# Conv stage: q product in the image's natural order, bias data on ScalarE's queue, bias and value products among the energies

## The chip, the core and the metric

One core of a Trainium2 chip runs the whole program. The metric is the device time of one execution, in microseconds, as the median of several runs. TensorE (PE in the rows) multiplies; its weight loads are the rows PEld. VectorE is DVE, ScalarE is ACT, GpSimd is POOL, and SyncE (SP) only issues DMAs here. ScalarE issues a few DMAs too.

## What is computed

The input is `x`, 4 images of 128 channels and 16 x 16 pixels. A convolutional attention comes first, then an attention over tokens with 8 heads, then a dense mixture of 8 experts. Only the first stage is touched:

```
q = einsum('bchw,oc->bohw', x, wq) + bq          # 16 channels
k = einsum('bchw,oc->bohw', x, wk) + bk          # 16 channels
v = einsum('bchw,oc->bohw', x, wv) + bv          # 128 channels
qf, kf = q.reshape(b, 16, h*w), k.reshape(b, 16, h*w)
energy = einsum('bci,bcj->bij', qf, kf).reshape(b, h, w, h, w)
attn = softmax(energy, axis=-1)
out  = einsum('bchk,bhwkv->bcwv', v, attn)
x    = gamma * out + x
```

(The literal reshape of the reference is `(b, c // 8, h * w)`, with c // 8 = 16.) All later stages need the result of this one.

## The kernel before

The program is written out by hand, one instruction stream for each engine, with semaphores between them. What stands in a stream in a row runs in that order; there is no scheduler. So the order on an engine is the order of the code in that engine's block.

The tokens of all images lie side by side, 1024 columns; a half `p` (512 columns) is two images. `x_sb` is the input with the channels on the partitions, in natural order, row `h` outside and column `w` inside. `dev` holds at first a second copy of the input in another order, for the values.

The stage goes like this:

- SyncE issues the loads: the two halves of `x_sb` (L282), the value bias `bv_sb` (L283, one row of 128 numbers sent to all 128 partitions), `dev`, the constants, the attention weights, then the experts' weights. ScalarE issues `convw_sb`, the weights of the three products (L414), `convb_sb`, the biases of q and k (L415), and `gamma_sb` (L416, one number sent to 128 partitions).
- TensorE first runs `turn`, matmuls on zeros whose result nobody reads (L855, 128x512, type f32r). Then, for each half, it makes the q product (L863, 16 output channels on PSUM partitions 64 to 79) and two k products (L867, PSUM partitions 0 to 15 and 32 to 47). L863 reads `x_sb` with `w` outside and `h` inside, so neighbouring columns of the product are 16 numbers (64 bytes) apart in `x_sb`. The last L867 of a half signals `proj_done`.
- ScalarE and VectorE copy the products out of PSUM and add the bias. Both wait for `convb_in` once and for `proj_done` of the half. ScalarE writes q for the first row group (L425), then k (L427). VectorE writes k (L585), waits for ScalarE's q copy of the half (`act_cq_ready`), and writes q for the second row group (L588).
- `conv_bias(i)` (L898) is the product that puts the value bias into PSUM bank 4 + i, `energy(q)` (L878) makes 16 products of one quarter of the energies, and `conv_values(i)` (L887) adds four value products to bank 4 + i. `energy(0)` waits for all copies of q and k; `conv_bias(0)` waits for `bv_in`; `conv_values(0)` waits for `xk_in`, the data in `dev`.
- The softmax of a quarter q: VectorE takes the maximum (L595) and subtracts it (L597), ScalarE takes the exponential (L431), VectorE sums (L603) and inverts (L606); GpSimd scales quarters 0 to 2 (L333), VectorE scales quarter 3 (L611). ScalarE copies the values out of PSUM (L522) between its exponentials.
- `conv_apply(0)` and `conv_apply(1)` (L910) multiply values and attention. The first needs the copied values and GpSimd's quarter 1, the second needs `last_A_ready`, VectorE's L611. L632 then makes the stage's output.

Most matmuls here are fp32, and the profile has two records for each fp32 matmul.

Of the kernel before, what the change touches and what calls it, by code (L numbers as in the profile page):

```python
# [19 lines left out]
B, C, H, W = 4, 128, 16, 16  # L20
# [4 lines left out]
C8 = C // 8  # L25
# [6 lines left out]
WQ, W4 = 4, 4  # L32
# [10 lines left out]
def hybrid_program(nc, x_in, xk_in, convw, convb, bv, gamma, attw, gate, w1, w2, b1, b2, consts, out):  # L43
# [5 lines left out]
    with ExitStack() as ctx:  # L49
        def sb(name, shape, dt=f32):  # L50
            return ctx.enter_context(nc.sbuf_tensor(name, shape, dt))

        def sem(name):
            return ctx.enter_context(nc.semaphore(name))
# [7 lines left out]
        convw_sb = sb("convw_sb", [128, QK + C])  # L62
        convb_sb = sb("convb_sb", [96 + C8, 1])
        bv_sb = sb("bv_sb", [128, C])
# [16 lines left out]
        x_sb = sb("x_sb", [128, T])  # L81
# [16 lines left out]
        cq = room[0:32 + C8, 5120:7168].rearrange("p (b w h k) -> p b w h k", b=B, w=W, h=H)  # L98
# [45 lines left out]
        PS = ctx.enter_context(nc.psum_tensor("PS", [128, 8, 512], f32))  # L144
# [5 lines left out]
        convb_in, bv_in, czero, tzero = sem("convb_in"), sem("bv_in"), sem("czero"), sem("tzero")  # L150
# [40 lines left out]
        def cols(p):  # L191
            return slice(p * HALF, (p + 1) * HALF)

# [75 lines left out]
        def weigh_visit(n):  # L272

            for k in range(VISITS):
                if n == MT * k + WEIGH_LAG - 2 * (k > E):
                    return k
            return None

        @block.sync
        def _(sp):  # L280
            for p in range(NHALF):
                sp.dma_start(x_sb[:, cols(p)], x_in[:, cols(p)]).then_inc(x_in_s[p], 16)  # L282
            sp.dma_start(bv_sb[:, :], bv.partition_broadcast(128)).then_inc(bv_in, 16)  # L283
            sp.dma_start(dev[:, :], xk_in).then_inc(xk_in_s, 16)
            sp.dma_start(cst[:, :], consts).then_inc(cst_in, 16)
            sp.dma_start(attw_sb[:, :], attw).then_inc(attw_in, 16)

            for e in range(2):
                sp.dma_start(w1raw[e][:, :], w1[:, e * HID:(e + 1) * HID]).then_inc(w1_in[e], 16)

            sp.dma_start(gate_sb[:, :], gate).then_inc(cst_in, 16)
            sp.dma_start(b2_sb[:, :], b2).then_inc(cst_in, 16)
            sp.dma_start(b1_sb[:, :], b1).then_inc(cst_in, 16)

            def comb_everywhere(p, part):

                if part == 0:
                    sp.wait_ge(combT_ready, p + 1)
                    sp.dma_start(comb_rows_dram[p], combT[:, cols(p)]).then_inc(comb_out, 16)
                    sp.wait_ge(comb_out, 16 * (p + 1))  # L300
                for e in range(E)[part * E // 2:(part + 1) * E // 2]:
                    if p:
                        sp.wait_ge(part_ready, e + 1)
                    sp.dma_start(combB[:, e, :], comb_rows_dram[p, e, :].partition_broadcast(128))\
                        .then_inc(combB_in[e], 16)

            for e in range(2, E):
                sp.dma_start(w1raw[e][:, :], w1[:, e * HID:(e + 1) * HID]).then_inc(w1_in[e], 16)
            for n in range(2):
                half = slice(n * E // 2, (n + 1) * E // 2)  # L310
                sp.dma_start(w2_sb[:, half, :], w2[:, half, :]).then_inc(w2_in[n], 16)
            for p in range(NHALF):
                comb_everywhere(p, 0)
                comb_everywhere(p, 1)

            for p in range(NHALF):
                sp.wait_ge(acc_done, E * (p + 1))
                sp.dma_start(out[:, cols(p)], t2[:, cols(p)]).then_inc(out_sent, 16)
            sp.wait_ge(out_sent, 16 * NHALF)
# [92 lines left out]
        @block.scalar  # L412
        def _(act):
            act.dma_start(convw_sb[:, :], convw).then_inc(convw_in, 16)  # L414
            act.dma_start(convb_sb[:, :], convb).then_inc(convb_in, 16)  # L415
            act.dma_start(gamma_sb[:, :], gamma.partition_broadcast(128)).then_inc(gamma_in, 16)  # L416

# [4 lines left out]
            for p in range(NHALF):  # L422
                act.wait_ge(proj_done, p + 1)
                pair = slice(2 * p, 2 * p + 2)
                nc.scalar.activation(cq[0:C8, pair, :, :, 0].rearrange("c b w h -> c (b w h)"), PS[64:64 + C8, p, :],  # L425
                                     ACT.Identity, bias=convb_sb[64:64 + C8, 0:1]).then_inc(act_cq_ready, 1)
                nc.scalar.activation(ck[32:32 + C8, pair, :], PS[32:32 + C8, p, 0:TOK].rearrange("c (b n) -> c b n", b=2),  # L427
                                     ACT.Identity, bias=convb_sb[32:32 + C8, 0:1]).then_inc(ck_ready, 1)
# [146 lines left out]
        def _(dve):  # L575
# [6 lines left out]
            for p in range(NHALF):  # L582
                dve.wait_ge(proj_done, p + 1)
                pair = slice(2 * p, 2 * p + 2)
                nc.vector.tensor_scalar(ck[0:C8, pair, :], PS[0:C8, p, 0:TOK].rearrange("c (b n) -> c b n", b=2),  # L585
                                        convb_sb[0:C8, 0:1], None, ALU.add).then_inc(ck_ready, 1)
                dve.wait_ge(act_cq_ready, p + 1)
                nc.vector.tensor_scalar(cq[32:32 + C8, pair, :, :, 1].rearrange("c b w h -> c (b w h)"),  # L588
                                        PS[64:64 + C8, p, :], convb_sb[64:64 + C8, 0:1], None, ALU.add)\
                    .then_inc(cq_ready, 1)  # L590

            def shift(q):
# [220 lines left out]
            for n in range(STEPS):  # L813
# [12 lines left out]
                k = weigh_visit(n)  # L826
# [22 lines left out]
        def _(pe):  # L849
            mm = nc.tensor.matmul  # L850

            def turn(count, bank=6):

                for _ in range(count):
                    mm(PS[:, bank, :], spin[:, 0:128], spin, start=True, stop=True)  # L855
# [4 lines left out]
            for p in range(NHALF):  # L860
                pe.wait_ge(x_in_s[p], 16)
                x2 = x_sb[:, cols(p)].rearrange("c (b g n) -> c g b n", b=2, g=K2N)
                mm(PS[64:64 + C8, p, :].rearrange("c (b w h) -> c b w h", b=2, w=W),  # L863
                   convw_sb[:, 0:C8], x_sb[:, cols(p)].rearrange("c (b h w) -> c b w h", b=2, h=H),
                   start=True, stop=True)
                for g in range(K2N):
                    last = mm(PS[32 * g:32 * g + C8, p, 0:TOK].rearrange("c (b n) -> c b n", b=2), convw_sb[:, C8:QK],  # L867
                              x2[:, g], start=True, stop=True)
                last.then_inc(proj_done, 1)

            def energy(q):
                if q == 0:
                    pe.wait_ge(act_cq_ready, NHALF)
                    pe.wait_ge(cq_ready, NHALF)
                    pe.wait_ge(ck_ready, 2 * NHALF)
                for w in range(W4):
                    for b in range(B):
                        last = mm(PS[32 * b:32 * (b + 1), q, w * K8 * W:(w + 1) * K8 * W],  # L878
                                  cq[:, b, W4 * q + w, :, :].rearrange("c h k -> c (h k)"), ck[:, b, :],
                                  start=True, stop=True)  # L880
                last.then_inc(energy_done, 1)

            def conv_values(i):
                if i == 0:
                    pe.wait_ge(xk_in_s, 16)
                for k in range(4 * i, 4 * i + 4):
                    last = mm(PS[:, 4 + i, (k % 4) * C:(k % 4 + 1) * C], x_k[:, k, :], convw_sb[:, QK:QK + C],  # L887
                              start=False, stop=True, skip_group_check=True)
                    if k % 4 == 1:
                        turn(1)  # L890
                last.then_inc(vT_done, 1)

            def conv_bias(i):

                if i == 0:
                    pe.wait_ge(share_ready, 1)
                    pe.wait_ge(bv_in, 16)
                mm(PS[:, 4 + i, :].rearrange("p (a c) -> p a c", c=C), share[:, :],  # L898
                   bv_sb[:, :].unsqueeze(1).broadcast_to([128, 4, C]), start=True, stop=False, skip_group_check=True)
# [289 lines left out]
                mm(y, w2h[e][:, ms], Gl[:, n % GR, :], start=False, stop=(m == MT - 1)).then_inc(down_done, 1)  # L1189


            turn(1)
            for i in range(2):
                conv_bias(i)
            for q in range(WQ):
                energy(q)
                turn(1)
            for i in range(2):
                conv_values(i)
            turn(2)  # L1200
            conv_apply(0)
            turn(1, 0)
            conv_apply(1)
# [134 lines left out]
```

## Time and profile before

| | |
|---|---|
| runs | 186.39 us median of 3 (186.04 to 187.66) |
| profiled execution | 186.13 us, of it 184.2 us span |
| TensorE busy | 174.1 us, 95% of the span |
| VectorE, ScalarE, GpSimd busy | 117.1, 123.2, 79.5 us |
| the conv stage | from the start to L632 at 23.29 us |

The span is what the trace covers; 1.93 us lie around it. Times of rows count from the start of the span. A busy share says how often an engine had something to do, not whether the end waited for it: for that there is the chain of work that ended last.

### The profile page before, as it was taken

How to read it: one execution, taken by the hardware profiler on the slowest of the kernel's cores; microseconds unless marked ns; L12 is line 12 of the kernel's file. 1: busy time of each engine (PE TensorE's matmuls, PEld its weight loads, DVE VectorE, ACT ScalarE, POOL GpSimd, SP SyncE). 2: the span in 40 equal slices, each digit the busy share in tenths (PEclk: the TensorE clock that was granted, in tenths of full speed). 3: DMA queues.
4: the chain of work that ended last, by engine and by line, in shares of the span. 5: the costliest groups of instructions: out<-in, count | busy, mean ns of one | idle time of the engine just before them, and what ended most of it. 6: DMA issues, size and time to landing. Idle time of an engine off the chain costs nothing.

```text
span 184.2 us, 3336 instructions
## 1 busy us (share of the span) xinstructions
PE 174.1 (95%) x1277; PEld 118.6 (64%) x1277; DVE 117.1 (64%) x199; ACT 123.2 (67%) x185; POOL 79.5 (43%) x68
## 2 busy tenths in 40 slices
PE   6999999989898998999999999999999999999991
PEld 3267867665466544447466567567887888888880
DVE  1569544985465396456084959397888677676673
ACT  3516953317727743545988598867878999999970
POOL 8404228988703284452536093524151152333312
PEclk9999999999999999999999999999999999999999
DMA  5799200000000000570000000000000880000001
GB/s 141 276 374 419 96 0 0 4 0 4 0 5 0 2 0 4 181 271 7 0 0 5 0 0 0 4 0 0 0 7 4 244 269 0 0 4 0 0 0 57
DMA packets 5791, 10.94 MB, mean 59 GB/s; under 512 B 1280, under 2 KB 1664, under 8 KB 5520
## 3 DMA queue, kind: packets, MB, share of 16 engines
q1 hardware_dynamic: 5360, 10.65, 16.7%
q8 instruction: 10, 0.16, 0.3%
q10 hardware_dynamic: 416, 0.08, 0.3%
q14 instruction: 5, 0.04, 0.1%
HBM read 10.17 MB, written 0.56 MB: 58 GB/s over the span
## 4 chain that ended last, share of the span: by engine, by line
PE 73%; issue 8%; ACT 7%; POOL 4%; DVE 4%; DMA 2%; ACTq 0%; DVEq 0%; POOLq 0%
PE PS L1159 9%; PE PS L1163 7%; PE PS L1160 7%; PE PS L1186 6%; PE PS L1189 6%; PE PS L1187 6%; PE PS L1181 4%; POOL pairs L357 4%; PE PS L1017 3%; PE PS L1031 3%; ACT room L516 2%; PE PS L910 2%; PE PS L878 2%; PE PS L1104 2%; DMA convw_sb<-convw 2%
## 5 line engine op out<-in xcount | busy, mean ns | idle before, releaser
L516 ACT ACTIVATE room<-PS,b_sb 128x512 f32<-128x512 f32 x64 | 43.6, 688 | 22.6 <-PE PS L1163 21.2
L772 DVE TENSOR_TENSOR Gl<-room,Gh 128x512 fp32r<-128x512 f32 x50 | 41.2, 831 | 13.7 <-ACT Gh L461 13.0
L365 POOL TENSOR_TENSOR x_sb<-x_sb,room 128x512 f32<-128x512 f32 x15 | 23.6, 1572 | 56.0 <-DVE room L781 56.0
L1159 PE MATMUL PS<-x2h,w1h 128*128 128x512 f32 x64 | 27.4, 427 | 1.2 <-ACT room L516 0.8
L461 ACT ACTIVATE Gh<-room 128x512 fp32r<-128x512 f32 x40 | 25.3, 633 | 1.3
L1163 PE MATMUL PS<-x2l,w1h 128*128 128x512 f32 x64 | 25.5, 398 | 0.0
L1160 PE MATMUL PS<-x2h,w1l 128*128 128x512 f32 x64 | 25.2, 393 | 0.0
L1186 PE MATMUL PS<-Gh,w2h 128*128 128x512 f32 x50 | 20.8, 416 | 0.0
L1187 PE MATMUL PS<-Gh,w2l 128*128 128x512 f32 x50 | 19.8, 395 | 0.0
L1189 PE MATMUL PS<-Gl,w2h 128*128 128x512 f32 x50 | 19.7, 395 | 0.0
L1159 PEld LDWEIGHTS PS<-x2h,w1h 128*128 128x128 f32 x64 | 12.0, 187 | 10.6 <-issue 4.9
L348 POOL TENSOR_TENSOR w2l<-w_sb,w2h 128x512 fp32r<-128x512 f32 x8 | 10.2, 1279 | 12.6 <-ACT w2h L455 12.6
L357 POOL TENSOR_TENSOR pairs<-shared_probs 128x512 f32<-128x512 f32 x10 | 13.7, 1390 | 4.6 <-ACT shared_probs L503 4.6
L1163 PEld LDWEIGHTS PS<-x2l,w1h 128*128 128x128 f32 x64 | 12.0, 188 | 3.5 <-DVE x2l L718 0.6
L682 DVE TENSOR_REDUCE other_nmx<-PS 128x4 f32<-128x1024 f32 x8 | 9.8, 1224 | 6.7 <-PE PS L1031 6.7
L1181 PE MATMUL PS<-room,w_sb 128*128 128x512 f32 x28 | 14.0, 592 | 0.0
L1160 PEld LDWEIGHTS PS<-x2h,w1l 128*128 128x128 f32 x64 | 12.0, 188 | 2.0
L767 DVE CAST Gh<-room 128x512 fp32r<-128x512 f32 x10 | 4.4, 444 | 13.5 <-ACT room L516 13.5
L503 ACT ACTIVATE shared_probs<-PS 128x1024 f32<-128x1024 f32 x12 | 11.6, 1022 | 1.9 <-PE PS L1074 1.7
L781 DVE SCALAR_TENSOR_TENSOR room<-PS,b_sb,room 128x512 f32<-128x512 f32 x16 | 11.9, 744 | 0.7 <-PE PS L1189 0.7
L373 POOL TENSOR_TENSOR ny<-nv,half_power 128x2 f32<-128x2 f32 (+1 forms) x6 | 4.9, 811 | 15.1 <-DVE nv L651 14.4
L1187 PEld LDWEIGHTS PS<-Gh,w2l 128*128 128x128 f32 x50 | 9.4, 188 | 2.6 <-issue 0.5
(136 smaller groups left out, 294.2 us busy)
## 6 DMA issues: line engine op xcount, KB each, us to landing
room<-comb_rows SPq DMA_DIRECT2D x16, 256.0 KB, 5.2
w1raw<-w SPq DMA_DIRECT2D x8, 256.0 KB, 5.9
w_sb<-w SPq DMA_DIRECT2D x2, 1024.0 KB, 10.6
x_sb<-x SPq DMA_DIRECT2D x2, 256.0 KB, 3.2
dev<-xk SPq DMA_DIRECT2D x1, 512.0 KB, 6.3
out<-x_sb SPq DMA_DIRECT2D x2, 256.0 KB, 4.2
attw_sb<-attw SPq DMA_DIRECT2D x1, 320.0 KB, 6.8
cst<-consts SPq DMA_DIRECT2D x1, 228.5 KB, 6.5
```

What stands on the lines that cost most here:

```text
L357: nc.gpsimd.tensor_tensor(pairs[:, u % 2, j, :], probs_of(u)[:, j, 0, :], probs_of(u)[:, j, 1, :], ALU.add).then_inc(paired, 1)
L365: nc.gpsimd.tensor_tensor(t2[:, cols(p)], t2[:, cols(p)], part[:, s, :], ALU.add).then_inc(acc_done, 1)
L461: nc.scalar.activation(Gh[:, n % GR, :], G[:, n % GR, :], ACT.Copy)\
L516: nc.scalar.activation(G[:, n % GR, :], PS[:, U_BANK[n % 2], :], ACT.Gelu, bias=b1_sb[:, c:c + 1])\
L772: nc.vector.tensor_tensor(Gl[:, n % GR, :], G[:, n % GR, :], Gh[:, n % GR, :].bitcast(f32), ALU.subtract)\
L1159: mm(o, w1h[e][:, ms], x2h[:, cols(p)], start=True, stop=False)
L1160: mm(o, w1l[e][:, ms], x2h[:, cols(p)], start=False, stop=False)
L1163: mm(o, w1h[e][:, ms], x2l[:, cols(p)], start=False, stop=True).then_inc(up_done, 1)
L1181: mm(y, w2_sb[:, e, ms], G[:, n % GR, :], start=(m == 0), stop=(m == MT - 1)).then_inc(down_done, 1)
L1186: mm(y, w2h[e][:, ms], Gh[:, n % GR, :], start=(m == 0), stop=False)
L1187: mm(y, w2l[e][:, ms], Gh[:, n % GR, :], start=False, stop=False)
L1189: mm(y, w2h[e][:, ms], Gl[:, n % GR, :], start=False, stop=(m == MT - 1)).then_inc(down_done, 1)
```

## The change

Four things are edited. (1) The q product reads `x_sb` in natural order, all 512 columns next to each other; the copies L425 and L588 read PSUM by columns in exchange, `w` outside and `h` inside, through the new helper `by_columns`. What they write, and where, stays the same. (2) The load of `bv_sb` goes from SyncE's stream to ScalarE's, between those of `convw_sb` and `convb_sb`. (3) `conv_bias(1)`, `conv_values(0)` and `conv_values(1)` stand among the energies, instead of ahead of and behind them. (4) The `turn` matmuls are set anew, and those within `conv_values` are gone.

```diff
+        def by_columns(images):
+
+            return images.rearrange("c (b h w) -> c b w h", b=2, h=H)
...
-            sp.dma_start(bv_sb[:, :], bv.partition_broadcast(128)).then_inc(bv_in, 16)
...
             act.dma_start(convw_sb[:, :], convw).then_inc(convw_in, 16)
+            act.dma_start(bv_sb[:, :], bv.partition_broadcast(128)).then_inc(bv_in, 16)
             act.dma_start(convb_sb[:, :], convb).then_inc(convb_in, 16)
...
-                nc.scalar.activation(cq[0:C8, pair, :, :, 0].rearrange("c b w h -> c (b w h)"), PS[64:64 + C8, p, :],
+                nc.scalar.activation(cq[0:C8, pair, :, :, 0], by_columns(PS[64:64 + C8, p, :]),
                                      ACT.Identity, bias=convb_sb[64:64 + C8, 0:1]).then_inc(act_cq_ready, 1)
...
-                nc.vector.tensor_scalar(cq[32:32 + C8, pair, :, :, 1].rearrange("c b w h -> c (b w h)"),
-                                        PS[64:64 + C8, p, :], convb_sb[64:64 + C8, 0:1], None, ALU.add)\
+                nc.vector.tensor_scalar(cq[32:32 + C8, pair, :, :, 1], by_columns(PS[64:64 + C8, p, :]), convb_sb[64:64 + C8, 0:1], None, ALU.add)\
                     .then_inc(cq_ready, 1)
...
-                mm(PS[64:64 + C8, p, :].rearrange("c (b w h) -> c b w h", b=2, w=W),
-                   convw_sb[:, 0:C8], x_sb[:, cols(p)].rearrange("c (b h w) -> c b w h", b=2, h=H),
-                   start=True, stop=True)
+                mm(PS[64:64 + C8, p, :], convw_sb[:, 0:C8], x_sb[:, cols(p)], start=True, stop=True)
...
-                    if k % 4 == 1:
-                        turn(1)
```

On TensorE, from the q and k products of the second half to the value products, there stood before (x_sb,convw_sb are the q and k products, x2h `turn`, bv_sb,share `conv_bias`, room the energies, convw_sb,dev the values):

```order
L867 MATMUL PS<-x_sb,convw_sb 16x256 x2
L855 MATMUL PS<-x2h 128x512
L898 MATMUL PS<-bv_sb,share 128x512 x2
L878 MATMUL PS<-room 32x128 x16
L855 MATMUL PS<-x2h 128x512
L878 MATMUL PS<-room 32x128 x16
L855 MATMUL PS<-x2h 128x512
L878 MATMUL PS<-room 32x128 x16
L855 MATMUL PS<-x2h 128x512
L878 MATMUL PS<-room 32x128 x16
L855 MATMUL PS<-x2h 128x512
L887 MATMUL PS<-convw_sb,dev 128x128 x2
```

At the same place in the changed kernel, whose line numbers differ by a few, stands:

```order
L868 MATMUL PS<-x_sb,convw_sb 16x256 x2
L858 MATMUL PS<-x2h 128x512 x2
L897 MATMUL PS<-bv_sb,share 128x512
L858 MATMUL PS<-x2h 128x512 x2
L879 MATMUL PS<-room 32x128 x16
L858 MATMUL PS<-x2h 128x512
L879 MATMUL PS<-room 32x128 x16
L897 MATMUL PS<-bv_sb,share 128x512
L879 MATMUL PS<-room 32x128 x16
L888 MATMUL PS<-convw_sb,dev 128x128 x4
L879 MATMUL PS<-room 32x128 x16
L888 MATMUL PS<-convw_sb,dev 128x128 x4
```

Ahead of the first energy there is one bias product less and three `turn` more; the second bias product and the first four value products have moved between the energies.

On ScalarE the stream begins, before, with:

```order
L414 DMA convw_sb<-convw 128x160
L415 DMA convb_sb<-convb 112x1
L416 DMA gamma_sb<-gamma 128x1
L419 ACT_TABLE_LOAD
L419 ACTIVATE table<-table 1x1
L425 ACTIVATE room<-PS,convb_sb 16x512
```

And now with:

```order
L417 DMA convw_sb<-convw 128x160
L418 DMA bv_sb<-bv 128x128
L419 DMA convb_sb<-convb 112x1
L420 DMA gamma_sb<-gamma 128x1
L423 ACT_TABLE_LOAD
L423 ACTIVATE table<-table 1x1
L429 ACTIVATE room<-PS,convb_sb 16x512
```

The load of the value bias stands ahead of that of the biases that the copies wait for.

## Rows read from the trace of the kernel before

**Rows 1.** Chain of work that ended last: start us, us, what.

```profile
4.08 0.61 PE PS L863
...
5.97 1.69 PE PS L863 x2
7.67 0.43 PE PS L855
8.10 1.72 PE PS L898 x4
9.82 1.01 PE PS L878 x32
...
16.24 0.89 PE PS L887 x8
...
18.50 2.07 PE PS L910 x64
...
21.06 2.07 PE PS L910 x64
```

**Rows 2.** All instructions of line 863: duration ns min/median/max, first and last start.

```profile
L863 PE MATMUL PS<-x_sb,convw_sb x4: 1033/1036/1041, 4.1 to 6.6; 128*16 128x512 f32 x4
```

**Rows 3.** Timeline of the weight loads: start us, us, engine, line, what.

```profile
4.61 0.10 PEld L867 LDWEIGHTS PS<-x_sb,convw_sb 128*16 128x16 f32 x2 [0.40 <-issue]
```

**Rows 4.** Timeline of ScalarE and VectorE, copies of q and k.

```profile
6.12 0.76 ACT L425 ACTIVATE room<-PS,convb_sb 16x512 f32<-16x512 f32 x1 [2.49 <-PE PS L867]
6.90 0.47 ACT L427 ACTIVATE room<-PS,convb_sb 16x256 f32<-16x256 f32 x1
7.74 0.71 ACT L425 ACTIVATE room<-PS,convb_sb 16x512 f32<-16x512 f32 x1 [0.37 <-remote]
...
6.14 0.47 DVE L585 TENSOR_SCALAR room<-PS,convb_sb 16x256 f32<-16x256 f32 x1 [4.57 <-PE PS L867]
6.91 0.75 DVE L588 TENSOR_SCALAR room<-PS,convb_sb 16x512 f32<-16x512 f32 x1 [0.30 <-ACT room L425]
...
8.48 0.75 DVE L588 TENSOR_SCALAR room<-PS,convb_sb 16x512 f32<-16x512 f32 x1 [0.27 <-ACT room L425]
```

**Rows 5.** DMA issues on the sequencers of ScalarE and SyncE: start us, us.

```profile
1.18 0.45 ACTq L415 DMA_DIRECT2D convb_sb<-convb  x1
1.65 0.45 ACTq L416 DMA_DIRECT2D gamma_sb<-gamma  x1
...
1.65 0.42 SPq L283 DMA_DIRECT2D bv_sb<-bv  x1
```

**Rows 6.** DMA view, 0 to 20 us: KB, us from issue to landing.

```profile
convw_sb<-convw ACTq DMA_DIRECT2D x1, 80.0 KB, 3.3
bv_sb<-bv SPq DMA_DIRECT2D x1, 64.0 KB, 5.5
convb_sb<-convb ACTq DMA_DIRECT2D x1, 0.4 KB, 3.6
gamma_sb<-gamma ACTq DMA_DIRECT2D x1, 0.5 KB, 5.7
```

**Rows 7.** DMA queues, 3.9 to 6.3 us: packets, MB, share of 16 engines.

```profile
q1 hardware_dynamic: 154, 0.19, 41.9%
q10 hardware_dynamic: 130, 0.00, 3.0%
```

**Rows 8.** Busy time by stretch: PE, PEld, DVE, ACT, POOL, clock, DMA share, GB/s.

```profile
10.90:20.90 10.00, 9.77 (x185) 7.55 (x185) 9.67 (x17) 6.07 (x11) 3.17 (x3) 1.00 0.89 350
```

**Rows 9.** Timeline of VectorE and GpSimd in the softmax.

```profile
14.65 0.63 DVE L595 TENSOR_REDUCE cmax<-PS 128x32 f32<-128x512 f32 x1
...
16.90 0.63 DVE L595 TENSOR_REDUCE cmax<-PS 128x32 f32<-128x512 f32 x1
...
20.20 0.71 DVE L611 TENSOR_TENSOR room<-room,crcp 128x512 f32<-128x512 f32 x1
...
17.06 1.06 POOL L333 TENSOR_TENSOR room<-room,crcp 128x512 f32<-128x512 f32 x1 [1.19 <-DVE crcp L606]
```

More of the change, by code:

```diff
@@ L1189, in down @@
                 mm(y, w2h[e][:, ms], Gl[:, n % GR, :], start=False, stop=(m == MT - 1)).then_inc(down_done, 1)
+            turn(2)
+            conv_bias(0)
+            turn(2)
+            energy(0)
             turn(1)
[L1193 to L1200, printed above, removed]
+            energy(1)
+            conv_bias(1)
+            energy(2)
+            conv_values(0)
+            energy(3)
+            conv_values(1)
+            turn(3)
             conv_apply(0)
```

## The prediction

> **What bounds the kernel now.** I first read the chain of work that ended last, because TensorE's busy share alone doesn't say where the end waits. In the first 10 us it runs through TensorE without a hole: from 4.08 us, when `convw_sb` has landed, through the q products to 7.67, one `turn` to 8.10, two bias products to 9.82, and there the first energy starts [rows 1]. Next I read the copies, since the energies wait for them: the last one, VectorE's second L588, starts at 8.48 and takes 0.75, so it ends at 9.23 [rows 4]. The first energy therefore starts 0.6 us after its data are there: TensorE is what sets it.
>
> After it VectorE sets the pace, which the chain hides because TensorE is kept busy. From 10.9 us, when the first quarter of the energies is done, to 20.9 VectorE is busy 9.67 of 10.00 us [rows 8], and its last row there, L611, ends at 20.91; `conv_apply(1)` starts at 21.06 [rows 1, 9]. So the stage is a front part that ends with `energy(0)`, and 10 us of VectorE's work hung to its end. What the change is worth is the shift of the first energy's start, which I call E0, now 9.82.
>
> **The q product.** Its four records take 1.04 us each by their duration, but they are pipelined; their pace is 1.69 us for two, 0.85 each [rows 1, 2]. A record of the same 512 columns in fp32 that are read in a row, L898, has a pace of 1.72 / 4 = 0.43 [rows 1]. The difference is the 64-byte step, since L863 runs alone from 5.97 on and is no faster there. With natural order I take 0.43: 4 x 0.43 = 1.72 in place of 3.4. The k products cost nothing now: they write other PSUM partitions and run beside L863. If they did not (they are 8 records of half the columns, 8 x 0.21 = 1.7), the sum would be 3.4 again, the cost of before, and that is the other bound; I take the cover as given. The second half's input is there by 4.61, when the second half's weight loads go [rows 3], and its q product is due at 4.08 + 0.86 = 4.94: no wait. So the products end near 5.8, and the copies, which were released 0.2 to 0.35 us behind the products, could start at 5.2 and 6.0.
>
> **TensorE's sum to E0.** 5.80, two `turn` 0.86, one bias product 0.86, two `turn` 0.86: 8.4. That is 1.4 earlier than 9.82. The bias product wants `bv_in` at 6.66; with the 5.5 us of now behind an issue at 1.18 it lands at 6.7 [rows 5, 6], so this holds within 0.1.
>
> **The copies' sum to E0.** Let t0 be the time at which ScalarE and VectorE may start. Both halves are then ready or nearly so, and the copies run back to back: ScalarE q 0.76, k 0.47, q 0.71, with its gaps of 0.02 that makes 1.98; then VectorE's q of the second half with a handover of 0.05 and 0.75, together 2.8 [rows 4]. So the last copy ends at t0 + 2.8, and E0 is t0 + 2.85, or 8.4 if that is later. They break even with the kernel of before at t0 = 6.97.
>
> **What t0 is.** This is where the change adds a wait. The copies wait for `convb_in` too. It lands now at 1.18 + 3.6 = 4.8, well ahead of the products [rows 5, 6]. With `bv_sb` issued ahead of it on ScalarE's queue the issue moves to 1.65, and its packets stand behind 128 packets of 512 bytes. On its sequencer the extra issue costs 0.45, which also delays the table load; that ends at 4.1 instead of 3.6 and hides behind the wait for the products. Queued behind the wait for `convb_in` are all copies on both engines, and TensorE waits for those. The lower bound of the landing is 1.65 + 3.6 = 5.25, if the transfer ahead costs nothing. For the upper bound there is a row: the third DMA of this queue, now `gamma_sb`, lands at 1.65 + 5.7 = 7.35, and `convb_sb` becomes the third [rows 5, 6]. From 3.9 to 6.3 us both queues crawl: 284 packets in 2.4 us, ScalarE's queue (q10) using 3% of the engines [rows 7]. `bv_sb` and `gamma_sb`, both one row sent to 128 partitions, are under way then, and take 5.5 and 5.7 us where the others ahead take 3.3 to 3.6. Neither end is nearer by its form, a tiny DMA of distinct rows behind a slow broadcast, so I take the middle, 6.3. Then E0 = 6.3 + 2.85 = 9.15 and the gain 9.82 - 9.15 = 0.67.
>
> In the Trainium skill, page "DMA: Bandwidth & Descriptors", the sections on queues and on issuing engines say that the queues of SyncE and ScalarE share the same 16 engines, that each engine takes a ring's descriptors in order, and that a second issuing engine saves only issue time. By that rule `bv_sb` gains nothing by its new queue and `convb_sb` stands fully behind it: t0 would be at the upper bound, 7.35, and the time that of the second rival. No row before shows that order directly; the slow third DMA of [rows 6] is in line with it.
>
> **The copies' price.** They read PSUM with a step of 64 bytes. No row here shows a strided PSUM read by ScalarE or VectorE. From below: nothing, since both engines' cost is now nearly all elements at about 1.05 ns (0.76 and 0.47 us for 512 and 256 elements, 0.75 and 0.47 on VectorE [rows 4]) and those copies already write every second number; a gain is excluded, because their reads are in a row now. From above: the step doubles the element part as it doubled that of the q product, 512 x 1.05 = 0.54 a copy. Between them: a stepped number takes these engines as long as it takes TensorE, 0.85 us for 512, which is 0.31 more than their 0.54. Three such copies stand in the chain to E0, so 0 to 1.6 us, by the middle value 0.9. The nearest row in form is these copies' own stepped write, which costs no more a number than L427's and L585's write in a row does; it is a write, and to SBUF, but by the same engines and of the same numbers. By it I take 0, and keep the rest for a rival.
>
> On this the Trainium skill, "PSUM — Partial Sum Buffer", section Specifications, says that PSUM has lines of 8 bytes and that a non-contiguous pattern slows matmuls; it has no price for the other engines' reads. If it held for them, it would be the third rival.
>
> **The energies and what moved between them.** Counted from E0, `energy(2)` is done at 1.01 + 0.43 + 1.01 + 0.86 + 1.01 = 4.3; VectorE asks for it at 14.65 - 9.82 = 4.8 [rows 1, 9]. `energy(3)` follows values of 0.89 and is done at 6.2, asked for at 16.90 - 9.82 = 7.1. `conv_values(1)` ends at 7.1, three `turn` at 8.4; before, `conv_apply(0)` started at 18.50 - 9.82 = 8.7, and GpSimd's quarter 1 is ready at 17.06 + 1.06 - 9.82 = 8.3. So `conv_apply(0)` starts at 8.4 at best, ends at 10.5, and `conv_apply(1)` still waits for L611, 11.1 after E0. All these moves cost nothing and give nothing; their cover is VectorE's 10 us. Were that cover gone, the second bias product would cost its 0.86. For the loads on SyncE's queue, each moves up one place and lands no later; none is waited for here.
>
> **Sum.** 186.13 - 0.67 = 185.46 for the profiled execution. That execution stands 0.26 under the median of the runs, so against the median: 186.39 - 0.67 = 185.7. One per cent is 1.86 us, about what a measurement of this kernel can tell from no change.
>
> **Rivals.**
> - First: TensorE sets E0. `convb_sb` lands before 5.6, as it does if the broadcast ahead delays it little (3.6 us to land for it now speak for that). E0 = 8.4, gain 1.4: 185.0. This is the most that the change can give.
> - Second: the landing is at 7.35 or later. E0 = 10.2, loss 0.4: 186.8. For it speaks the third DMA's own landing; against it, that `gamma_sb` is itself slow in form.
> - Third, on the other side: the strided read of PSUM costs. With t0 = 6.3, E0 is 9.15 + 3c for a price c of each copy; from c = 0.22 on the kernel is slower. At the full 0.54, E0 = 10.8, loss 1.0: 187.4; with the late landing, loss 2.0: 188.4. At the 0.31 of TensorE's pace, E0 = 10.1 and the time 186.7. For it speaks what the same step does to TensorE's reads; against it, the free stepped writes of these engines.
> - Fourth: the q product doesn't get faster, because the k products then no longer fit beside it. The products end at 7.5, TensorE's sum is 10.1, loss 0.3: 186.7.
>
> **How the numbers follow.** Forecast 0.38; first rival 0.19; second 0.17; third 0.20; fourth 0.06. Faster by over 1% needs a gain of 1.86, more than any case gives: 0.04 for what I have missed. Slower by over 1% needs both the late landing and the full price of the stride: 0.06. Within 1%: 0.90. For the range, 185.0 less the runs' spread of 0.2 is the low end, 184.8; the third rival's 187.4 is the high end, and beyond lies only the double case.
>
> **What would show it.** The q product's records a pace of 0.43, and the products over near 5.8; the first L429 (L425 before) starts not with the products but with the DMA of `convb_sb`, at 6.3 in a range of 5.25 to 7.4; the q copies still take 0.75; TensorE idles between its `turn` and the first energy; VectorE from the first L595 to its last scaling takes the same 10.0 us. I am wrong if the first copy starts at 5.3, if the q copies take over 0.9, or if VectorE has holes between the quarters.

## The result, and the profile after

The changed kernel takes 193.13 us, median of 6 runs (191.49 to 193.25), the kernel before 186.37, median of 6: ratio 1.0342, 95% interval [1.0312, 1.0372]. It is 6.8 us slower, outside the range that I gave. The profiled execution has a span of 191.3 us against 184.2, so 7.1 us are to be found. In some kernels below, and in the kernel before, single executions took over 1.5% longer than the fastest of the same kernel, with a lower granted clock; the ratios leave those out, and the text gives their count.

The head of the page of the kernel after, with the row of TensorE's granted clock in 40 slices of 4.8 us (tenths of full speed, 9 being 90% or more):

```profile
span 191.3 us, 3334 instructions
...
PEclk9975589999999999999999999999999999999998
```

In the third to sixth slice the clock is down. The busy time by stretch says how far; the columns are those of [rows 8], the clock is the third number from the end:

```profile
10.90:20.90 10.00, 9.83 (x115) 6.43 (x119) 5.89 (x11) 2.49 (x5) 1.05 (x1) 0.55 0.86 339
12.10:25.10 13.00, 13.00 (x121) 9.20 (x118) 8.36 (x14) 3.55 (x7) 2.15 (x3) 0.50 0.57 225
```

All through these 13 us TensorE ran at half speed, the lower of its two levels, 1.2 in place of 2.4 GHz; the trace's list of clock changes has the fall at 11.96 and the rise at 25.62 us, 13.65 us later. In the stretch in which VectorE was busy 9.67 of 10.00 us [rows 8] it is busy 5.89: it is no longer the engine that is waited for.

The chain of work that ended last, in the kernel after (start us, us, what), stands against [rows 1]:

```profile
1.65 6.52 DMA convb_sb<-convb
...
8.19 0.72 ACT room L429
...
10.22 0.76 DVE room L592
...
11.07 1.13 PE PS L879 x32
12.20 0.72 PE PS L858
12.92 1.86 PE PS L879 x32
14.79 2.00 PE PS L897 x2
...
25.77 2.00 PE PS L909 x64
...
28.20 2.03 PE PS L909 x64
...
30.39 0.49 DVE t L635
```

It begins with the load of the q and k biases, not with TensorE, and the first energy starts at 11.07 instead of 9.82: 1.25 us. From there to the stage's output it was 23.29 - 9.82 = 13.47 us and is 30.39 - 11.07 = 19.32: 5.85 us more, and in this part an energy takes 1.86 instead of 1.01 and a bias product 2.00 instead of 0.86 (1.05 to 1.10 where one stands alone between other work at full clock, as below). The two sum to the 7.1 us. The new order has no part in the 5.85: in the first run below, which has this order at full clock, the same stretch is 22.86 - 9.39 = 13.47 us again. Everything behind the stage is as before.

Where the delay of 1.25 is from, the timeline of the kernel after shows:

```profile
6.22 0.60 PE L866 MATMUL PS<-x_sb,convw_sb 128*16 128x512 f32 x1 [0.66 <-DMA x_sb<-x]
...
8.19 0.71 ACT L429 ACTIVATE room<-PS,convb_sb 16x512 f32<-16x512 f32 x1 [4.08 <-DMA convb_sb<-convb]
...
8.94 0.75 DVE L592 TENSOR_SCALAR room<-PS,convb_sb 16x512 f32<-16x512 f32 x1 [0.27 <-ACT room L429]
...
11.07 1.13 PE L879 MATMUL PS<-room 48*32 48x128 f32 x32 [1.83 <-DVE room L592]
```

And the issues of the DMA view, as [rows 6] (KB, us from issue to landing):

```profile
bv_sb<-bv ACTq DMA_DIRECT2D x1, 64.0 KB, 5.4
convb_sb<-convb ACTq DMA_DIRECT2D x1, 0.4 KB, 6.5
gamma_sb<-gamma ACTq DMA_DIRECT2D x1, 0.5 KB, 7.1
```

The biases land at 8.17, and all eight copies wait for that. TensorE stands idle for 0.66 us ahead of the second half's product, whose data now come at 6.2 instead of 4.6 [rows 3], and for 1.83 us ahead of the first energy. The clock falls 0.9 us after the end of the second of these stretches. The theory to test (A) was: the late biases make TensorE idle, and the idle stretch brings the clock down. The rivals: (B) the new order on TensorE brings it down, (P) the natural product does, (C) the data's delay or the stepped PSUM reads themselves are the loss.

### The profile page after: what moved, and what is told of

Its sections match the earlier page's. It is cut to its first block, busy times and chain, and to the rows that moved or that the text cites. A ratio compares the mean times of both kernels' runs of the same rounds, so it can differ in the third digit from the quotient of the medians.

```text
span 191.3 us, 3334 instructions
## 1 busy us (share of the span) xinstructions
PE 179.1 (94%) x1276; PEld 122.2 (64%) x1276; DVE 117.5 (61%) x199; ACT 123.1 (64%) x185; POOL 79.4 (41%) x68
## 4 chain that ended last, share of the span: by engine, by line
PE 71%; issue 8%; ACT 6%; DVE 5%; POOL 4%; DMA 3%; ACTq 0%; DVEq 0%; POOLq 0%
PE PS L1158 8%; PE PS L1162 7%; PE PS L1159 7%; PE PS L1185 6%; PE PS L1188 5%; PE PS L1186 5%; PE PS L1180 4%; POOL pairs L360 4%; PE PS L879 4%; DMA convb_sb<-convb 3%; PE PS L1016 2%; PE PS L1030 2%; ACT room L520 2%; PE PS L909 2%; PE PS L888 2%
```

## The experiments

### The value bias back on SyncE's stream

```diff
+            sp.dma_start(bv_sb[:, :], bv.partition_broadcast(128)).then_inc(bv_in, 16)
             sp.dma_start(dev[:, :], xk_in).then_inc(xk_in_s, 16)
...
-            act.dma_start(bv_sb[:, :], bv.partition_broadcast(128)).then_inc(bv_in, 16)
```

> The changed kernel with the load of the value bias back on SyncE's stream, between the input and dev; all else stays. Theory A (the value bias ahead of the q and k biases on ScalarE's queue delays these, TensorE then has nothing to do for 1.8 us, and the granted clock falls to half for 13 us): the biases land near 4.8, the products end near 5.8, TensorE has no hole over 0.6 us, the granted clock stays 1.00, the first energy starts at 8.9 to 9.2 and the time is 185.3 to 185.9. Theory B (the clock falls because of the new order on TensorE, with fewer and shorter stretches of turn ahead of and between the energies): the clock falls here too, time 191 or more. Theory C (the stepped PSUM reads or the new order cost by themselves): 187 to 188 at full clock.

Measured: 185.72 us, ratio to the kernel before 0.9973 [0.9955, 0.9992]; the clock held in 5 of 5 executions. One moved DMA is worth 7.4 us by the medians. B, P and the half of C on the stepped reads are gone in their plain form, since the new order, the natural product and those reads are in here. The chain of this kernel:

```profile
7.14 0.66 PE PS L858 x2
...
7.82 1.10 PE PS L897 x2
8.92 0.47 PE PS L858 x2
9.39 1.01 PE PS L879 x32
```

The products ended near 7.1, not 5.8 (see the eighth run), the bias product waited for its data to 7.82, and the first energy starts 0.43 us ahead of that of before. That is the whole gain.

### The two loads swapped on ScalarE's queue

```diff
-            act.dma_start(bv_sb[:, :], bv.partition_broadcast(128)).then_inc(bv_in, 16)
             act.dma_start(convb_sb[:, :], convb).then_inc(convb_in, 16)
+            act.dma_start(bv_sb[:, :], bv.partition_broadcast(128)).then_inc(bv_in, 16)
```

> The changed kernel with the two loads swapped on ScalarE's queue: weights, q and k biases, value bias, gamma. Theory A: the q and k biases land near 4.8, but the value bias still runs beside the second half of the input, which lands as late as 6.2 as in the changed kernel; the products end near 7.1, the last copy near 9.0, TensorE stands on its own work at 9.7 and the time is 186.0 to 186.6, with the clock at 1.00. If the half of the input lands at 4.6, as before the change, 185.0 to 185.5. Theory B: the clock falls, 191 or more.

Measured: 186.11 us, ratio 0.9985 [0.9952, 1.0019], clock held in 10 of 10. The q and k biases land after 4.0 us instead of 6.5, the first copy starts at 5.49. So it is the place ahead of them, not the queue, that did the harm. Now the value bias is the late one, 6.5 us after its issue:

```profile
8.30 1.10 PE L897 MATMUL PS<-bv_sb,share 128*128 128x512 f32 x2 [1.30 <-DMA bv_sb<-bv]
```

An idle stretch of 1.30 us, and the clock held.

### Four more turn ahead of the first energy

```diff
-            turn(2)
+            turn(6)
             energy(0)
```

> The changed kernel with six turn instead of two right ahead of the first energy; the late data stay. The four added ones (4 x 0.43 = 1.7 us) fill the hole from 9.24 to 11.04. Theory A: the first energy starts at 11.1 as in the changed kernel, the granted clock stays 1.00, and only the delay is left: 186.4 + 1.25 = 187.6 (187.2 to 188.2), so 5.5 of the 6.8 us are the clock. Theory B: the clock falls all the same between the energies, 192 to 193.

Measured: 192.92 us, ratio 1.035 [1.0305, 1.0394], the clock fell in 4 of 4. Theory A had said 187.6 with the clock held, so this was a miss. I had sized the cover wrongly. The six turn with the bias product ahead of them were over at 9.38, because a turn behind a turn takes about 0.23 us here (next run), and a stretch of 1.46 us stayed empty:

```profile
10.84 1.08 PE L879 MATMUL PS<-room 48*32 48x128 f32 x32 [1.46 <-DVE room L592]
```

So this run didn't test what it was made for; the next one does.

### Fourteen turn

```diff
-            turn(2)
+            turn(14)
             energy(0)
```

> The changed kernel with fourteen turn instead of two right ahead of the first energy. The run before this one showed that a turn behind a turn takes only about 0.22 us there, so its six turn ended at 9.38 and left a hole of 1.46. Fourteen fill it up to 10.8 or a little beyond the last copy. Theory A (the idle stretch ahead of the first energy brings the clock down): granted clock 1.00, first energy at 10.9 to 11.4, time 187.2 to 188.0. Theory B (the late data and the new order bring it down together, whatever TensorE does meanwhile): clock 0.50 for some 13 us, time 192 to 193.3.

Measured: 188.19 us, ratio 1.0107 [1.0084, 1.0131], clock held in 4 of 4. In its profile the biases landed even later, at 8.5, and the energies started at 11.68, but TensorE was busy all the while: fourteen turn in 3.78 us, of which the last 0.4 is the run-out of the last one. The stretch 12 to 25 us of the runs with six and with fourteen turn, in this order:

```profile
12.00:25.00 13.00, 13.00 (x118) 8.94 (x118) 8.35 (x14) 3.85 (x7) 2.45 (x3) 0.50 0.57 225
```

```profile
7.97 3.78 PE L858 MATMUL PS<-x2h 128*128 128x512 f32 x14
...
12.00:25.00 13.00, 12.65 (x276) 9.76 (x268) 9.69 (x17) 7.88 (x14) 3.17 (x3) 1.00 0.57 226
```

The same late data, the same order, the same product, and work that nobody reads in the hole: 4.9 us faster than the changed kernel by the medians. Theory A holds for the bulk. What is left here is about 2 us (1.0107), and not all of it is the price of the late data, which the next run puts at 1.0 us. In this profile the biases landed 0.34 us later than in the kernel after, and the last copy ended at 11.31: the energies could have started at 11.4 and waited for the turn until 11.68. Cover that is too long costs time too.

### The kernel before with the bias load moved

```diff
-            sp.dma_start(bv_sb[:, :], bv.partition_broadcast(128)).then_inc(bv_in, 16)
...
             act.dma_start(convw_sb[:, :], convw).then_inc(convw_in, 16)
+            act.dma_start(bv_sb[:, :], bv.partition_broadcast(128)).then_inc(bv_in, 16)
```

> The kernel before with one edit: the value bias is loaded by ScalarE, ahead of the q and k biases. Theory A: the q and k biases land near 8.2, the copies end near 11.0, TensorE's own work ends near 10.1, so it has a hole of 0.9 us, half of that of the changed kernel. Time at least 186.4 + 1.25 = 187.6 if the clock holds, 191 to 193 if it falls. Theory B: no fall of the clock, since the order on TensorE is the old one, and 187.6 at most. A rival that the queue's order doesn't matter: 186.4.

Measured: 187.26 us, ratio 1.0053 [1.0033, 1.0073]; the clock fell in one of four executions (191.9 us). In the profiled execution, which held, the first energy starts at 11.08 behind an idle stretch of 1.24. With two bias products to do, TensorE has more cover than in the kernel after, and the move with the clock held cost 1.0 us, a little under the 1.25 that the theory had as its least.

### The natural product alone, and the order alone

The first of the two makes the edits at L425, L588 and L863 and nothing else; the second makes only these:

```diff
-            turn(1)
-            for i in range(2):
-                conv_bias(i)
-            for q in range(WQ):
-                energy(q)
-                turn(1)
-            for i in range(2):
-                conv_values(i)
-            turn(2)
+            turn(2)
+            conv_bias(0)
+            turn(2)
+            energy(0)
...
```

with the rest of the order as in the change, and without the turn in `conv_values`.

> The kernel before with the q product in natural order and the copies by columns, and nothing else. Theory S (the 64-byte step doubles the pace of the product): its records go at 0.43, the products end near 5.9, the bias products wait for their data until 7.2, the first energy starts near 9.0, time 185.4 to 185.8. Theory L (TensorE works at its low level until some time between 4.5 and 7.5 us in all kernels, since its first turn have a pace of 0.43 and later ones of 0.22, and the step costs nothing): the products' pace is 0.85 up to that time whatever the order, and the time is that of the kernel before within 0.4 us.

> The kernel before with TensorE's new order alone: one bias product and two and two turn ahead of the first energy, the other products among the energies. If the order costs and gives nothing, as predicted: first energy between 9.0 and 9.8, time 185.6 to 186.5. If the new order is what costs: over 187.

Measured: 185.96 us, ratio 0.998 [0.9948, 1.0012], and 185.93 us, ratio 0.9989 [0.9978, 0.9999]. None of the 20 executions took the long fall of the kernel after. One of the natural product took 187.55 us at a mean granted clock of 0.990, where the others of both kernels have 0.995 to 1.00; the longest of the new order is 186.16. Neither edit costs anything; for the product that is what theory L had, and not S (185.4 to 185.8). The natural product alone gained nothing that can be told: its records had a pace of 0.83 to 0.85 us in that profile, as long as the stepped ones.

### Both reads where TensorE has been busy for long

```diff
             for q in range(WQ):
                 energy(q)
                 turn(1)
+                if q in (1, 2):
+                    extra(q == 2)
```

`extra` is one more q product of the first half, written to bank 7: stepped as at L863 behind the second energy, natural behind the third.

> The kernel before with two more q products of the first half, written to an unused bank, whose result nobody reads: one with the 64-byte step behind the second energy, one in natural order behind the third, where TensorE has been busy for long. Theory S: the stepped one has a pace of 0.85 for a record, the natural one 0.43. Theory L: both 0.43.

Measured: 189.04 us in one execution, the only one, with the clock at 1.00. Its chain (L1200 is the stepped, L1198 the natural product, two records each):

```profile
12.88 1.80 PE PS L1200 x2
...
16.12 0.96 PE PS L1198 x2
```

The step does double the pace here: 0.90 against 0.48 us for a record, 0.84 and 0.44 by the starts of the two records. Here theory S was right, for the first products of the kernel theory L: both were half right. In its first microseconds TensorE works at half pace in every profile: its first turn follow each other at 0.43 us, later ones at 0.23, though the column of the granted clock reads 1.00. The trace's list of clock changes begins with a rise to 1.00, at 7.35 us in the kernel before, at 5.14 in the kernel after, and from 4.66 to 7.70 over all fourteen profiles; the column takes what lies ahead of it as 1.00. Ahead of the rise natural and stepped records both take 0.83 to 0.85; behind it the natural ones take 0.43 to 0.48 and the stepped ones stay at 0.84 to 0.90 (0.85 also in the first products of the two kernels of the next section, where the rise came at 5.00 and 5.19). In the kernel after, the second half's records start at 6.22 and 6.67, 0.45 apart. The product's gain is therefore only what lies behind the rise. I can't say what sets the time of the rise: there is one profile of each kernel. In the Trainium skill, page "SBUF — State Buffer", section "Door 1: The DMA port swizzle", an access that goes to a new 16-byte line each time is said to pay a penalty; these two rows agree, at the higher level alone.

### Everything but the product, with and without turn

The first kernel is the one before with the bias load moved and the new order. The second leaves out the two and two turn ahead of the first energy as well:

```diff
-            turn(2)
             conv_bias(0)
-            turn(2)
             energy(0)
```

> The kernel before with the value bias on ScalarE's queue ahead of the q and k biases and with TensorE's new order, but with the old stepped product: everything of the change but the product. Theory A (the length of TensorE's idle stretch ahead of the first energy decides on the clock): the products end at 7.6, the turn and one bias product at 9.5, the last copy at 11.0, so a hole of about 1.5 us, between the 1.24 that mostly passed and the 1.46 and 1.83 that always brought the clock down: the clock falls in most runs, 191 to 193.2. Theory P (the faster natural product, which lets TensorE run dry earlier, is needed for the fall): clock 1.00 and 187.2 to 187.6.

> The kernel before with the bias load moved and the new order, stepped product, and without the two and two turn ahead of the first energy. TensorE ends its bias product near 9.1 or earlier, so the idle stretch grows from 1.46 to between 2.0 and 2.6. Theory A: the clock falls in nearly all executions, 191.5 to 193.5. Theory P (with the stepped product the clock holds): 187.2 to 187.6.

Measured: 187.41 us, ratio 1.0051 [1.0016, 1.0086], the clock fell in one of four (193.21 us); and 193.28 us, ratio 1.0407 [1.037, 1.0443], fell in 6 of 6. The rows of the first energy, of one kernel and of the other:

```profile
11.16 0.97 PE L878 MATMUL PS<-room 48*32 48x128 f32 x28 [1.46 <-DVE room L588]
```

```profile
11.37 0.75 PE L878 MATMUL PS<-room 48*32 48x128 f32 x20 [2.74 <-DVE room L588]
...
12.00:25.00 13.00, 13.00 (x134) 8.95 (x125) 7.87 (x13) 3.01 (x5) 2.10 (x2) 0.50 0.57 225
```

In the first kernel theory A had the clock fall in most executions, and it missed; the time is theory P's. But the second rules out theory P in its plain form: with the old product and a hole of 2.74 us the clock fell each time, to the same 0.50 for the same 13 us. A profile with a hole of 1.46 belongs here to a kernel that fell in one of four executions, with the natural product to one that fell in four of four. That is a hint and no more: the executions are few, they were taken on different chips, and the hole is known of the profiled execution only, which here is one that held.

### Seven turn behind the natural product

```diff
-            turn(2)
+            turn(7)
             energy(0)
```

> The changed kernel with seven turn right ahead of the first energy. Two runs had the same idle stretch of 1.46 us: with the natural product the clock fell in 4 of 4 executions, with the stepped one in 1 of 4. Seven turn leave about 1.2 us (1.46 less 0.23), as long as the stretch in the kernel before with the bias load moved, where it fell in 1 of 4. Theory A (the length of the idle stretch decides): it falls in a minority of the executions, median 187.2 to 188.0. Theory P (the natural product, behind which TensorE has had less work at its high level, matters beside it): it falls in most, median 191 to 193.2.

Measured: 187.28 us, ratio 1.0069 [1.0056, 1.0081]; the clock fell in one of seven (191.51 us). That is what theory A had forecast. Between six and seven turn lies the change from four of four to one of seven, on different chips. The profile was taken of the execution that fell, and it doesn't fit a simple rule:

```profile
4.39 1.03 PE L866 MATMUL PS<-x_sb,convw_sb 128*16 128x512 f32 x1 [0.40 <-DMA convw_sb<-convw]
...
10.97 1.08 PE L879 MATMUL PS<-room 48*32 48x128 f32 x32 [0.38 <-DVE room L592]
```

Its last idle stretch is only 0.38 us, with 0.40 ahead of the first product. Its clock also rose later, at 6.81 us, and fell later, at 13.64, 2.7 us after the first energy had begun; in the other three profiles that fell the rise is at 5.14 to 5.19 and the fall at 11.96 to 12.01. No experiment held the time of the first rise fixed, and it is a rival to the length of the stretch. So which mix of idle stretches, turn, products and that time tips the clock stays open. What is shown is that more cover makes the fall rare and full cover ended it in all executions tried.

### A better version: both bias products behind two energies

The kernel of the first run, with this order:

```diff
-            turn(2)
-            conv_bias(0)
-            turn(2)
+            turn(7)
             energy(0)
-            turn(1)
             energy(1)
+            conv_bias(0)
             conv_bias(1)
             energy(2)
```

> The kernel of the first run (natural product, value bias on SyncE's queue) with both bias products moved behind the second energy and seven turn ahead of the first energy. In the first run the copies were done at 8.95 and the first energy started at 9.32 to 9.39, behind a bias product that had waited for its data until 7.8. Without that, and with turn of 0.22 as cover, the first energy starts at 9.0 to 9.1 and the time is 0.3 us below that of the first run: 185.3 to 185.5. The two bias products make the third energy end at 4.75 us behind the start of the first, VectorE wants it at 4.8; if that cover is too thin, the gain is eaten and the time stays at 185.7.

Measured: 185.59 us, ratio 0.9961 [0.9937, 0.9986], clock held in 6 of 6. It is the fastest kernel of the study, 0.6 us under the one before, but not to be told from the first run (0.9973). In its profile the products ended later, the last copy at 9.20, and the energies started at 9.37, so most of the expected 0.3 us didn't come. The later rise of the clock fits that: 7.30 us here, 6.43 in the first run's profile.

## Why the prediction was wrong

**The copies' wait (the term t0) was the right mechanism, mis-sized.** I took the landing at 6.3 between 5.25 and 7.35; it was 8.17. The upper bound came from the third DMA of ScalarE's queue before the change, and the third DMA there had nothing but small packets ahead of it. With the 64 KB of the value bias ahead and `dev` already running on the other queue, the same place in the queue lands 0.8 us later, and `gamma_sb` after 7.1 us instead of 5.7. The sum behind it was right to the hundredth: the copies run 8.19 to 10.98, 2.79 us, where I had 2.8. By my own terms a t0 of 8.19 gives a first energy at 11.04 and a loss of 1.2 us; it started at 11.07, 1.25 late. In the Trainium skill, page "DMA: Bandwidth & Descriptors", the section "Queues, rings and completion order" has each engine take a ring's descriptors in order; the first two experiments agree, with 6.5 us for the biases behind the value bias and 3.8 and 4.0 ahead of it. Whether the value bias gains by its queue they don't settle: it took 5.2 to 5.4 us second on ScalarE's queue, 5.5 to 6.1 third on SyncE's.

**The step that failed is TensorE's idle time, which I priced at nothing.** I wrote that TensorE would idle between its turn and the first energy, took only the shift, and had no case in which the clock falls. It was 5.85 of the 7.1 us. With my t0 of 6.3 the hole would have been 0.7 us and perhaps harmless; but the second rival's landing already opened one of 1.8, and there the price of the hole belonged in the sum. The same stretch at full clock takes 13.47 us and took 19.32. No row before showed the clock below 1.00, but one profile is one execution: of the 55 executions of the kernel before that were taken beside the experiments, 11 took 187.65 to 189.24 us at a mean granted clock of 0.977 to 0.991, the others at most 186.49 at 0.995 to 1.00. Where in them the clock was down isn't known. And the kernel had turn everywhere around its waits: those turn were the row that I should have read. In the Trainium skill, the page "TensorE: Matmul & The Clock Gate", section "Why this matters for your kernels", warns that gaps between bursts of matmuls bring TensorE back to its lower level. The trace agrees with the direction, 0.50 behind such a gap, and not with the size: the gaps of the page are longer than the 1.83 us here, and here the measurement decides.

**The turn were priced at 0.43; one behind another takes 0.23.** The 0.43 is the first one's, behind an fp32 product. So two and two turn fill 1.3 us and not 1.7, and the hole is wider than my sum had it. The same error spoiled the run with six.

**The product's gain was mis-read.** I said the 64-byte step is the difference between 0.85 and 0.43, since L863 was no faster alone. But L863 was being timed while TensorE worked at half pace, where the step costs nothing; its last record starts at 6.63 us, the rise is at 7.35, and L898 was timed behind it. The two causes look alike in one number. Alone, the edit gained 0 within [0.9948, 1.0012]. The second half's input also landed later, which I had not counted at all: its weight loads start at 5.3 to 6.2 us in the eight profiles with the value bias on ScalarE's queue and at 4.6 to 5.1 in the six with it on SyncE's. The 6.2 of the kernel after is the latest of them.

**What held.** The stepped PSUM reads cost nothing: ScalarE's q copies take 0.71 and 0.70 us, VectorE's 0.75, as in [rows 4]; the rule of the Trainium skill on PSUM lines ("PSUM — Partial Sum Buffer", section "Specifications (TRN2)") speaks of matmuls, and these reads show no cost. The moves among the energies cost nothing (0.9989 for the order alone). And at full clock the stage is VectorE's: in the run with fourteen turn it goes from quarter to quarter without a hole of note, 9.69 busy of 13 us with the tail of the stage included.

## What to carry to other kernels

When a change makes TensorE wait, price the wait twice: the shift itself, and the same stage at half clock, here 13.65 us of it and 5.85 us of time. A load that others queue behind belongs behind the small loads that many instructions wait for, whichever engine issues it. And before a record's pace is laid to its access pattern, look for a record of known cost in the same stretch: a column that reads full clock did not show the half pace of the first microseconds, the pace of the turn did.

## What the runs showed of the hardware that I had not expected

- The q and k biases, 0.4 KB, landed 6.3 to 6.9 us after their issue behind the value bias, and 3.6 to 4.0 us ahead of it.
- TensorE went to half pace, 0.50, 0.6 to 1.2 us after the first energy had begun in three profiles and 2.7 us after it in a fourth, that is while it was busy again, and stayed there for 13.65 us of full work, in the fourth for 10.24.
- The q product, 128x512 fp32 with a 64-byte step, took 0.90 us a record against 0.48 in a row when TensorE was at its higher level (0.84 and 0.44 by the starts), and 0.83 to 0.85 both ways before it.
- The granted clock first rose at 4.66 to 7.70 us, depending on the profile, and the column reads 1.00 ahead of it.
- By the stretch in the one profiled execution: of the kernels with 1.46 us one fell in 4 of 4 executions and another in 1 of 4, the one with 1.24 in 1 of 4, the one with 1.30 in none of 10, with 1.83 and 2.74 in 6 of 6 each, with 0.38 in 1 of 7. What else counts is open.
